# GpSimd's sends to the experts' slots: one at a time over thirteen half-slots, at TensorE's signal of the turned maxima, in place of rows of eight

## What is computed

```python
x = x + _L0_attn_ref(_layernorm(x, axis=-1), L0_attn_Wq, L0_attn_Wk, L0_attn_Wv, L0_attn_Wo)
x = x + _L0_ffn_ref(_layernorm(x, axis=-1), L0_ffn_w_router, L0_ffn_w1, L0_ffn_w2, L0_ffn_bias)
...
capacity = int(CAPACITY_FACTOR * TOP_K * T / E)
scores = jax.nn.softmax(xf @ w_router, axis=-1)
expert_weights, top_experts = jax.lax.top_k(scores, TOP_K)
...
xb = jnp.zeros((E * capacity + 1, hs), x.dtype).at[slot].set(xf[src])
h = jax.nn.gelu(jnp.einsum('ech,ehf->ecf', xb, w1))
y = jnp.einsum('ecf,efh->ech', h, w2).reshape(E * capacity, hs)
out = jnp.zeros((T, hs), x.dtype).at[src].add(flat_w[order][:, None] * yv)
```

## Time and profile before

| | us |
|---|---|
| median of three runs | 1073.68 |
| the profiled execution | 1073.41 |
| its span | 1071.7 |
| TensorE busy | 856.2 (80%) |
| VectorE busy | 520.4 (49%) |
| ScalarE busy | 438.8 (41%) |
| GpSimd busy | 354.0 (33%) |
| the sends, L349, 112 of them | 110.0, 982 ns each |
| TensorE's granted clock, mean | 0.84 |

### The profile page before, as it was taken

One profiled execution on the slowest core, in us unless ns is written; L12 is line 12 of the kernel. 1 busy time (PEld: TensorE's weight loads), 2 busy tenths in 40 slices (PEclk: granted clock), 3 DMA queues, 4 the chain that ended last, 5 costly groups with the idle time before them and its releaser, 6 DMA issues.

```text
span 1071.7 us, 18997 instructions
## 1 busy us (share of the span) xinstructions
PE 856.2 (80%) x7400; PEld 580.0 (54%) x7400; DVE 520.4 (49%) x1558; ACT 438.8 (41%) x884; POOL 354.0 (33%) x317
## 2 busy tenths in 40 slices
PE   3999999789779869877986997795039979889790
PEld 1455565355446535544653554453029968878690
DVE  3687878556556755755574565465102211211210
ACT  3455565363344525534442643431024434334230
POOL 2000001410330240033023003302536777877777
PEclk9999999786878976987797876685559989989895
DMA  3911001100100110010011001001132555555433
GB/s 106 392 58 46 11 7 38 35 14 6 48 27 6 43 35 9 6 48 27 6 45 32 8 6 48 26 6 48 44 102 26 94 92 76 74 91 95 73 34 33
DMA packets 48577, 54.19 MB, mean 51 GB/s; under 512 B 6001, under 2 KB 37384, under 8 KB 47472
## 3 DMA queue, kind: packets, MB, share of 16 engines
q0 software_dynamic: 22528, 17.22, 11.3%
q1 hardware_dynamic: 25968, 35.86, 10.1%
HBM read 17.70 MB, written 31.59 MB: 46 GB/s over the span
## 4 chain that ended last, share of the span: by engine, by line
PE 48%; issue 14%; POOL 12%; DVE 11%; another core or an unknown queue 8%; DMA 4%; ACT 3%; POOLq 0%; DVEq 0%; SPq 0%; ACTq 0%
POOL out L411 11%; PE sT_ps L1027 11%; PE u_ps L1052 6%; PE tail_ps L1036 5%; PE sT_ps L1044 4%; PE tail_ps L1067 3%; PE tail_ps L1072 3%; PE sT_ps L1021 3%; DMA out<-y_sb,xg 3%; PE o_ps L1061 3%; DVE kmax L632 3%; PE proj_ps L1002 2%; PE tail_ps L1085 2%; PE proj_ps L1003 2%
## 5 line engine op out<-in xcount | busy, mean ns | idle before, releaser
L411 POOL DMA_INDIRECT out<-y_sb,xg x128 | 198.8, 1553 | 81.4 <-DVE y_sb L962 42.4
L359 POOL TENSOR_TENSOR xbias<-x_sb,bias_sb 128x256 f32<-128x256 f32 x32 | 23.2, 724 | 574.5 <-DVE x_sb L667 574.5
L632 DVE TRANSPOSE_TENSOR_REDUCE kmax<-sT_ps 128x32 f32<-128x1024 f32 x128 | 159.5, 1246 | 58.0 <-PE sT_ps L1027 29.2
L483 ACT ACTIVATE probsT<-sT_ps 128x1024 f32<-128x1024 f32 x128 | 131.2, 1025 | 102.0 <-PE sT_ps L1044 96.7
L1027 PE MATMUL sT_ps<-qbd,kT 32*128 32x256 f32 x1024 | 170.1, 456 | 0.0
L564 ACT ACTIVATE hT<-sT_ps 128x512 f32<-128x512 f32 x128 | 76.5, 598 | 146.6 <-PE sT_ps L1230 138.9
L1027 PEld LDWEIGHTS sT_ps<-qbd,kT 32*128 32x128 f32 x1024 | 100.8, 213 | 45.4 <-issue 35.7
L349 POOL DMA_INDIRECT slots_dram<-send_rows,slot_id x112 | 110.0, 982 | 46.3 <-issue 32.9
L1230 PE MATMUL sT_ps<-xT_hl,w_hl 128*128 128x512 f32 x384 | 106.3, 430 | 21.4 <-DVE xT_hl L949 21.4
L1230 PEld LDWEIGHTS sT_ps<-xT_hl,w_hl 128*128 128x128 f32 x384 | 76.3, 206 | 38.5 <-issue 14.7
L1052 PE MATMUL u_ps<-probsT,v_sb 128*32 128x128 f32 x2048 | 95.9, 312 | 0.0
(11 more groups left out here) (131 smaller groups left out, 1180.2 us busy)
## 6 DMA issues: line engine op xcount, KB each, us to landing
slots_dram<-empty_rows SPq DMA_DIRECT2D x8, 1096.0 KB, 16.1
xg<-slots_dram SPq DMA_DIRECT2D x32, 274.0 KB, 2.8
out<-xbias SPq DMA_DIRECT2D x32, 128.0 KB
w_sb<-in_L_ffn_w SPq DMA_DIRECT2D x16, 256.0 KB
send_rows<-rows_sb SPq DMA_DIRECT2D x7, 548.0 KB, 3.0
out<-y_sb,xg POOLq DMA_INDIRECT x128
slots_dram<-send_rows,slot_id POOLq DMA_INDIRECT x112
out<-empty_rows SPq DMA_DIRECT2D x1, 1024.0 KB, 25.4
```

Source lines behind the costliest of these rows:

```text
L411: pool.indirect_dma_start(out=out, out_offset=bass.IndirectOffsetOnAxis(ap=xg[:, r, 4 * c + k, ROW - 1:ROW].bitcast(U32), axis=0), in_=y_s ...
L483: nc.scalar.activation(probsT[:, gp].rearrange("p b k h q -> p (b k h q)"), sT_ps[:, gp].rearrange("p b c -> p (b c)"), ACT.Exp).then_inc( ...
L632: nc.vector.tensor_reduce(kmax[:, u % 2, :], sT_ps[:, u % 2].rearrange("p b (c q) -> p (b c) q", q=32), AX.X, ALU.max, apply_transpose=Tru ...
```

## The change

`send` now calls a `send_tile` for one indirect DMA. A list `turns` is made of the half-slots (t, half) from (1, 1) to (7, 1), thirteen, with (3, 0), (5, 0) and (7, 0) once more: sixteen turns, one send each. In every half-slot GpSimd first waits for `s_maxT`, and then issues what stands at that turn. `leave` moves behind the second half's send in odd slots. The notice that all sends have landed (`s_sent`) moves from slot 6 to slot 0 of the next sequence, and after the last slot for sequence 7.

```diff
+            turns = [(t, half) for t in range(1, TILES) for half in range(2)][1:]
+            turns = sorted(turns + [(3, 0), (5, 0), (7, 0)])
+
+            def sends(b, t, half):
+
+                if (t, half) == turns[0]:
                     pool.wait_ge(s_send, START + 16 * (b - 1))
                     pool.sem_inc(s_turn_pool, 1)
-                if 1 <= t < 5:
-                    send(send_rows, range(2 * t - 2, 2 * t))
-                if t == 6:
-                    pool.wait_ge(s_scat, 16 * TOPK * TILES * (b - 1))
-                    pool.sem_inc(s_sent, 1)
-
-            def slot(b, t, first=False, second=False, last=False):
-                g = b * TILES + t
-                if t % 2 == 1 and not (first and t == 1):
-                    leave(b * PAIRS + (t - 3) // 2, early=first and t < 5)
-                if not (first or second):
-                    sends(b, t)
+                for n, turn in enumerate(turns):
+                    if turn == (t, half):
+                        send_tile(send_rows, n // 2, n % 2)
+
+            def sent(b):
+                pool.wait_ge(s_scat, 16 * TOPK * TILES * (b - 1))
+                pool.sem_inc(s_sent, 1)
+
+            def slot(b, t, first=False, second=False):
+                if t == 0 and b > 2:
+                    sent(b - 1)
+                for half in range(2):
+                    pool.wait_ge(s_maxT, 2 * (b * TILES + t) + half + 1)
+                    if not (first or second):
+                        sends(b, t, half)
+                    if t % 2 == 1 and half == 1 and not (first and t == 1):
+                        leave(b * PAIRS + (t - 3) // 2, early=first and t < 5)
```

More of the change, by code:

```diff
@@ L344, in late_constants, with send_tile @@
                           channel_multiplier=SPP).then_inc(c_pool, 1)
+            def send_tile(rows, j, k):
+                pool.indirect_dma_start(
+                    out=slots_dram,
+                    out_offset=bass.IndirectOffsetOnAxis(ap=slot_id[:, k, j:j + 1].bitcast(U32), axis=0),
+                    in_=rows[:, j, :],
+                    in_offset=None, bounds_check=E * CAP - 1, oob_is_err=False).then_inc(s_scat, 16)
             def send(rows, tiles):
@@ L348, in send @@
                     for k in range(2):
-                        pool.indirect_dma_start(
-                            out=slots_dram,
-                            out_offset=bass.IndirectOffsetOnAxis(ap=slot_id[:, k, j:j + 1].bitcast(U32), axis=0),
-                            in_=rows[:, j, :],
-                            in_offset=None, bounds_check=E * CAP - 1, oob_is_err=False).then_inc(s_scat, 16)
+                        send_tile(rows, j, k)
             def leave(n, early=False):
@@ L392, in _ @@
             for t in range(TILES):
-                slot(BATCH - 1, t, last=True)
+                slot(BATCH - 1, t)
+            sent(BATCH - 1)
             leave(NPAIR - 1)
```

2 lines of the change are left out of this document (removed).

## The result

| | us |
|---|---|
| before, median of 4 runs | 1079.22 |
| changed kernel, median of 4 runs | 1053.19 (1017.39 to 1084.59) |
| changed / before | 0.948, interval 0.932 to 0.963 |
| forecast | 974, range 943 to 1019 |

The change makes the kernel faster there, but the forecast is 79 us too low and its range misses. The four runs of the changed kernel lie 67 us apart, which itself wants a cause. In it L362 is `leave`, L347 the send, L645 the row maxima, L1049 the turned maxima, L1057 the shifts.

A forecast was written before the change was run, and what follows sets the result against it. TensorE was taken as the bound when undisturbed, its signals late beside close sends and its clock then lower. 1073.4 - 130.4 (rows gone) + 30.6 (spread sends) = 973.6, forecast 974 us, range 943 to 1019.

The forecast's parts named there:

- point 3: GpSimd's new wait for `s_maxT` in every half-slot: `leave` behind it goes about as before, no cost.
- the sum's 973.6: Whole kernel: profiled 1073.4 us less 130.4 for vanished rows plus 30.6 for spread sends, forecast as 974.
- 5 x 76.4: Expected sign: sequences 2 to 6 at about 76.4 us each, with a clock near 1.00.
- Point 5: VectorE's steps beside the sends: neither stretches the other, nothing taken.
- Point 1: Rows of eight sends vanish in sequences 2 to 7: 130.4 us saved if lone sends cost nothing.
- Point 2: Sixteen spread sends in the attention cost 5.1 us a sequence, 30.6 us in six, at most 76.
- Point 4: Notice of landed sends comes in slot 0 instead of slot 6: covered; otherwise a few us a sequence.
- the clock stays low: Rival: small TensorE stops in each slot lower the clock in two of four pairs, 58 us, 1032 us; chance 0.10.
- A fixed share for each send: Rival: each send blocks TensorE's signals wherever it stands; at 1.45 us a send, 1082 us; chance 0.05.
- Sends that bunch up: Rival: GpSimd comes late to its waits, so several sends go out 1.28 us apart; 1039 us; chance 0.02.
- Shifts and sends that hold each other up: Rival: each send adds 0.98 us to VectorE's steps between maxima and shifts; 1068 us with point 2; chance 0.03.

The follow-up runs named there:

- after_again: The changed kernel, unaltered, run a second time; median 1053.34 us, 0.989 of the kernel before.
- leave_ahead: The changed kernel with `leave` put ahead of GpSimd's wait for the second half's maxima, sends unchanged; 956.71 us, 0.886 of before, and 957.19 us when repeated.
- rows_of_eight_third: Third run of `leave_ahead` with each sequence's sixteen sends at two turns of eight; 957.68 us, 1.005 of before.
- gap_filled: `leave_ahead` with six idle matmuls added in TensorE's stops of slots 3 and 7; 953.45 us, 1.010 of before.
- first group: Runs on one chip where the kernel before took 1068.06 us: `after_again`, `leave_ahead`, `no_sends` and `before_leave_late`.
- prompt groups: The three groups of runs where the kernel before took 955, 964.5 and 958 us and TensorE's signals were prompt beside rows of eight sends.
- rows_of_eight: `leave_ahead` with each sequence's sixteen sends at two turns of eight, (1, 1) and (3, 1); 960.27 us, 1.011 of before.
- no_sends: `leave_ahead` without the 96 sends of sequences 2 to 7 and the waits for their landing; 952.73 us, 0.890 of before.
- late group: A group of runs where the kernel before took 1068 or 1073 us and TensorE's signals came late beside rows of eight sends.
- chains_spread: `leave_ahead` with VectorE's chain of small steps divided more evenly over three half-slots and three second-pick steps earlier; 952.66 us, 1.000 of before; repeated 951.51 us.
- rows_of_eight_fourth: Fourth run of `leave_ahead` with each sequence's sixteen sends at two turns of eight; 1082.59 us, 1.002 of before, which took 1072.51 us there.
- before_leave_late: The kernel before, rows of eight kept, with `leave` made to wait for the odd slot's second shifts; 1109.26 us, 1.039 of before.

## Why the forecast was wrong

**The step that failed is point 3**, "it goes about as before ... No cost" on `leave`. It measured 97 us, `after_again` against `leave_ahead`. I had looked at who waits for `leave`, and found no one near. What counted is beside whom it runs: behind the second half's send it lies on VectorE's chain of 0.17 us steps. The added time has this breakdown in the profile of `after_again`, 69 us above the sum's 973.6: sequences 2 to 6 take 426.9 us where 5 x 76.4 = 382 was forecast, +45; sequence 1 takes 81.8 for 71.3, +10.5; sequence 7 takes 76.9 for 72.3 (88.8 - 21.6 + 5.1), +4.6; and sequence 1 starts at 119.6 instead of 109.9, +9.7. That last item isn't the change's: `leave_ahead` starts it at 120.6 too, `rows_of_eight_third` at 109.8. Nor are the 10.5: some 2 are that the row ends at a `leave` which now stands later, and the rest is the fall at 162.9. `gap_filled`, whose `leave` is ahead, has 17 us at 1.2 GHz at the same place (151.3 to 168.3), and from the last residual of sequence 0 to that of sequence 1 it takes 77.9 us, the changed kernel 79.3 and before 71.4. One move, that of `leave`, brings the kernel to 956.7. That `leave`'s place is the cause of the 97 us is shown; that they come by way of the stops and the clock is shown in part, as below.

**Point 5 weighed the right rule against the wrong instruction.** I applied the section "Who interferes with whom" of the Trainium skill's page "SBUF — State Buffer" to the sends only, and was right that these stretch next to nothing: beside a send in `leave_ahead` L659 takes 0.42 and L627 0.17 us, and one instruction of VectorE in sequences 2 to 7 was longer, L724 with 0.45 us for 0.20. But `leave` moved as well; it is an addition with two inputs in SBUF, and beside it L627, L630, L694 and L654 take 0.70, 0.64, 0.75 and 0.72 us for 0.17, 0.17, 0.22 and 0.18. By that rule whichever of two comes second is held up; the trace agrees for L630 and L654, which begin behind `leave` and end with it, 0.5 us an instruction. It doesn't tell why L627 and L694, which begin some 0.6 us ahead of `leave`'s recorded start, beside the send, are stretched as well. In the changed kernel that happens only where a send stands directly ahead of `leave`, and no run looks into it. In the kernel before `leave` kept clear of those steps: VectorE's whole stretched time was 0.7 us, as in `leave_ahead`; it is 14 in the changed kernel.

**Point 1 was right where it applies.** The delays of rows of eight are gone, TensorE's signals are prompt beside a lone send, and the sequences of `leave_ahead` that stay undisturbed take 71.7 us. The 130.4 us were there in the main: 1068 to 957 in the first group is 111. In part they never were the rows': in sequences 2 to 6 of before's profile three falls, 48 us at 1.2 GHz and so by estimate up to 24 us lost, begin in slot 5, over 21 us behind the last stop. And the point rests on an effect that the three prompt groups do not show: there `rows_of_eight` takes 956 to 960 us.

**Point 2 was mis-sized.** It put 30.6 us on the spread sends. `leave_ahead` less `no_sends` is 4 us, and a sequence shows 0.4 us (71.7 against 71.3), not 5.1. In the profile of `after_again`, of a late group, an idle VectorE or ScalarE answers a TensorE instruction that ended beside a lone send 0.04 us later in the median and 0.31 at most, and beside the second send of a pair 0.05 and 0.29; in before's rows of eight it is up to 6.7. So the 0.8 us taken for a pair was at most 0.3, the 0.9 for the first send some 0.3 (L667), and the 0.4 for second halves was not there. The 27 us too many hid part of the other error.

**Point 4** has no run of its own; nothing in the times of `leave_ahead` and `no_sends`, 4 us apart, speaks for a cost.

**The rival that happened is that the clock stays low**, for another reason than I gave it. I had 1032 us for it, from small stops by sends. The stops are two a sequence, 2.2 (once 2.4) and 1.6 to 2.0 us, lengthened by `leave` from 1.2 and 1.3; and the 44 of 49 us by which sequences 2 to 6 exceed those of `leave_ahead` are TensorE's busy time. The sum had no term for what a stop of 2 us does to the clock, nor for the falls in slot 5, though the earlier trace rows held one of them, in a pair that TensorE filled to 23.86 of 24.00 us. In three profiles of the changed kernel the clock falls at 27 of 30 stops of 1.7 us and more; in `leave_ahead` at 3 of 11 of 1.2 to 1.4 us. That fits stops as the way from `leave` to the clock, but not for all of it: of some 160 us at 1.2 GHz in sequences 2 to 6 of `after_again` 51 us are falls in slot 5. The runs of the changed kernel scatter between 1012 and 1085 us as its clock does: the execution of 1042.97 us has a mean of 0.84, that of 1084.59 one of 0.79. The kernel that the forecast had in mind, `leave_ahead`, takes 957, within its range and 17 us under its 974; but where before takes 955 to 965 that is no gain, and the forecast had no such case. The Trainium skill's page "TensorE: Matmul & The Clock Gate", section "What's actually happening", has the throttled state as the default that activity lifts; the falls after stops fit, that of 370.1 us in `chains_spread`, behind 10 us without idle time, and the others in slot 5 do not fit easily.

The other three rivals fell. A fixed share for each send: 4 us for 96. Sends that bunch up: they stand 3.2 us and more apart, but for four gaps of 2.2, and the pairs 1.28. Shifts and sends that hold each other up: not seen beyond that one instruction.

Left open are two things. What makes some groups late and others prompt: the number recorded for the chip, 11, was the same in one group of each kind, so it is not simply the chip, and no cause was tried. And what lets the clock fall in slot 5, where TensorE did not stop; `chains_spread` and `gap_filled` left these falls as they were, and none of the runs changes the routing's matmuls that stand there. `chains_spread` has the lowest medians of the kernels that send all rows, 951.5 and 952.7, and was not run in a late group.

## What to carry to other kernels

When an instruction moves on an engine, ask not only who waits for it and what it waits for, but which small instructions on the neighbouring engine it will now lie beside; a hold-up of half a microsecond on the chain ahead of TensorE can cost far more than itself: here 14 us of them went with 97 us, most of it by the lower clock. Where one edit changes two things (here the spacing of sends and the place of `leave`), split them before judging: the spacing alone was worth up to 11% and the edit as made between 5% gained and 8% lost. Before blaming a fall of the clock on the stop before it, mark where in the loop each fall begins: a share of these came at a place without any stop. And time a kernel on several occasions before believing a stall in one profile, since this one's main stall was absent in three of five groups.

## What the runs showed of the hardware

- The kernel before took 1068 and 1073 us in two groups and 955, 965 and 958 in three, with the same instructions. What differs in the profiles of one kernel with rows of eight is whether TensorE's signals arrive late beside indirect DMAs of GpSimd 1.28 us apart: ScalarE answered 4.9 us late in `rows_of_eight_fourth` and 0.03 in `rows_of_eight_third`. Sends 2.2 us and more apart, and pairs, delayed them by 0.31 us at most in a late group (`after_again`).
- An addition of GpSimd on 128x256 with both inputs in SBUF (0.76 us) holds up a 0.17 us instruction of VectorE to 0.64 to 0.70 us; a CAST of 128x32 with one input too, 0.18 to 0.72. The issue of an indirect DMA (0.98 us) held up next to none: one instruction of 0.20 us to 0.45 in `leave_ahead`, five CASTs of 0.18 us to 0.33 to 0.47 in `before_leave_late`.
- Stops of TensorE of 1.7 to 2.4 us were followed by 7 to 31 us at 1.2 GHz at 27 of 30 places in three profiles of the changed kernel; stops of 1.2 to 1.4 us in `leave_ahead` at 3 of 11.
- The clock also fell without a stop, and then nearly always in the same half-slot: 5 times in `after_again` for 17 to 24 us, 22 to 31 us behind the last stop, and in `gap_filled`, which has no stop of 1 us in these sequences, 3 times for 7 to 17 us.
